# Moving the row sums of a sort's ranks from ScalarE into accumulating VectorE instructions

## The chip, the cores and the metric

One Trainium2 chip, one core of it. The metric is the device time of one execution of the whole kernel in microseconds (us), the median over the runs.

## The reference

12,500 nodes with 64 features and 200,000 edges (`src`, `dst` sorted by `dst`). Two graph layers follow each other, each behind a layer norm and a ReLU. Cut to what matters:

```python
# layer 0
aggr_msg = segment_sum(edge_attr_64, src, num_segments=12500)
x = x + relu(concat([h, aggr_msg]) @ W1 + b1) @ W2 + b2
# layer 1: attention over the edges of each destination
z = h @ W_fc.T
a = z[src] @ blk[0] + z[dst] @ blk[3] + ex @ w_e + (a constant of the moments of z[src], z[dst])
att = where(a > 0, a, 0.01 * a)
w = exp(att - segment_max(att, dst)[dst]); w = w / segment_sum(w, dst)[dst]
x = x + segment_sum(w[:, None] * (z[src] + ez), dst)
```

The change lies in layer 0. Its sum goes over `src`, and the edges are sorted by `dst`, so the kernel first sorts the edges' rows by source.

## The kernel before, in words

Edges are taken in 196 **macros** of 1,024 (128 partitions x `G` = 8 columns). A node is a pair of one of 98 blocks (`NB`) and a place in it. The macros fall into 8 chunks of 8, 20, 34, 38, 34, 26, 20 and 16 (`MS`). Within a chunk every edge gets a row number ("rank") in a sorted table in HBM. GpSimd (POOL) scatters the macro's 64-wide rows there by 8 indirect DMAs, one for each column (`scatter`, line 615). While chunk c is ranked and scattered, the sorted rows of chunk c-1 are read back by SyncE (SP) in groups of four tiles and summed: VectorE builds one-hots (`next_group`, line 1381), TensorE multiplies (`group`, line 990), VectorE adds the four results into `work` (`add`, line 1368). VectorE also builds one-hots to count chunk c+1 (line 1281, counted by TensorE at line 925), and ScalarE builds one-hot-like signs of the destinations (`destination_signs`, 8 + 8 activations at lines 723 and 725), which TensorE multiplies (line 968). All this is one straight-line program per engine, written out macro by macro.

The rank of a macro goes so:

1. TensorE leaves in PSUM (`ranks`, 128 x 8 x 98) a running count for each block (`advance`, lines 956 and 959, `s_rank`). It waits for VectorE's product of the macro before (`s_prod`), since it changes `ranks`.
2. VectorE multiplies `ranks` by the one-hot of each edge's block (`rank`, line 1299, one instruction of 784 columns, `s_prod`). The next instruction is the one-hot of the next macro (line 1281).
3. ScalarE sums each of the eight stretches of 98 products into one number (`rank_out`, line 707, eight activations with an accumulator output, `s_red`), waits for its own `s_red` and converts the eight sums to integers (line 710, `s_idx`). Before it writes `pos_f` and `idx` it waits until the scatter of four macros earlier has landed (`s_sc`).
4. ScalarE then copies the source numbers beside the edge rows (`row_sources`, line 715, `s_col`), and then does the destination signs.
5. POOL waits for `s_idx` and `s_col` and scatters.

`pos_f`, `idx` and `ea_sb` have four buffers, `prod` has two. VectorE waits in `rank(m)` for `s_red` of macro m-2, since it writes that product's buffer. Macro 0 alone is summed and converted by VectorE (lines 1303 and 1306). After the sort come the tail of the sums, the dense layers, and from about 3,000 us on the attention loop, in which POOL gathers (line 643). None of that is touched, but for the name of a semaphore in three waits.

Of the kernel before, what the change touches and what calls it, by code (L numbers as in the profile page):

```python
# [4 lines left out]
ALU = mybir.AluOpType  # L5
# [87 lines left out]
def gnn_kernel(nc, x, src, dst, e2, e64, W1, b1, W2, b2, W_fc, W_attn, W_edge, W_e2n, W_m1, W_m2, out):  # L93
    with ExitStack() as ctx:
# [168 lines left out]
        s_prod = sem("s_prod")  # L263
        s_red = sem("s_red")
        s_sc = [sem(f"s_sc{k}") for k in range(4)]
# [158 lines left out]
        def _(sp):  # L424
# [79 lines left out]
            sp.wait_ge(s_sp, N0)  # L504
            sp.wait_ge(s_red, NM)
            for i in range(GN[NCH - 1]):
# [149 lines left out]
        def _(act):  # L656
# [40 lines left out]

            def rank_out(m):

                if m == 0:  # L700
                    return
                act.wait_ge(s_prod, m + 1)
                if m >= 4:
                    act.wait_ge(s_sc[m % 4], 16 * G * (m // 4))
                for g in range(G):
                    at = prod[:, m % 2, g * NB:(g + 1) * NB]
                    ins = a_.activation(at, at, ACT.Copy, accum_out=pos_f[:, m % 4, g:g + 1])  # L707
                ins.then_inc(s_red, 1)
                act.wait_ge(s_red, m + 1)
                a_.activation(idx[:, m % 4, :], pos_f[:, m % 4, :], ACT.Copy).then_inc(s_idx, 1)  # L710

            def row_sources(m):
# [22 lines left out]
            for m in range(NM):  # L735
                if m in FILLS:
                    zero_fill(*FILLS[m])
                if m == 5:
                    act.wait_ge(s_dsub, 1)
                    a_.activation(squares_a, d_sb[:, :, :], ACT.Square).then_inc(s_sq, 1)  # L740
                if m == 8:
                    act.wait_ge(s_vv, 1)
                    a_.activation(var_sb[:, :], var_sb[:, :], ACT.Sqrt).then_inc(s_std, 1)
                if m == DST_FROM:
                    act.wait_ge(s_split, 3)
                    act.wait_ge(s_const, 2)
                if m == A0[2]:
                    act.wait_ge(s_tabi, 1)
                if m % 2 == 0 and 0 <= m - A0[2] < 18:
                    floor_fill((m - A0[2]) // 2)  # L750
                rank_out(m)
                row_sources(m)
                for d in DSTS.get(m, ()):
                    destination_signs(d)
# [455 lines left out]
        def _(dve):  # L1210
# [83 lines left out]
            def rank(m):  # L1294

                dve.wait_ge(s_rank, m + 1)
                if m >= 2:
                    dve.wait_ge(s_red, m - 1)
                v_.tensor_tensor(prod[:, m % 2, :].rearrange("p (h c) -> p h c", h=2), ranks,  # L1299
                                 ohs[:, m % 2, :].rearrange("p (h c) -> p h c", h=2), ALU.mult).then_inc(s_prod, 1)  # L1300
                if m == 0:
                    dve.wait_ge(s_prod, 1)
                    v_.tensor_reduce(pos_f[:, 0, :], prod[:, 0, :].rearrange("p (g j) -> p g j", g=G), X_AXIS, ALU.add
                                     ).then_inc(s_red, 1)
                    dve.wait_ge(s_red, 1)
                    v_.tensor_copy(idx[:, 0, :], pos_f[:, 0, :]).then_inc(s_idx, 1)
                if m + 1 < NM:
                    rank_onehots(m + 1)
# [245 lines left out]
            past = tmp_row[0:1, 0:n].rearrange("a (i u) -> a i u", u=GRP)  # L1554
            dve.wait_ge(s_red, NM)
            ch(v_.tensor_copy(past, at_first))
# [16 lines left out]
            dve.wait_ge(s_add, GRP * N0 + GN[NCH - 1])  # L1573
            dve.wait_ge(s_red, NM)
            dve.sem_inc(s_h, 1)
# [346 lines left out]
```

## Time and profile before

| | us |
|---|---|
| median of 3 runs | 5434.41 (5429.04 to 5434.47) |
| the profiled execution, its own time | 5417.05 |
| its span | 5415.2 |
| first rank product of VectorE (line 1299) starts / last starts | 32.4 / 2717.1 |
| VectorE busy / ScalarE busy / POOL busy / TensorE busy, share of the span | 55% / 41% / 56% / 42% |

Busy time is the union of an engine's instructions; "idle before" a group is what the engine waited ahead of it, and the arrow names what ended the wait. "remote" is a wait whose releaser the profile does not find. "issue" is time in which the engine waited for nothing that the profile shows.

### The profile page before, as it was taken

Reading aid. Unit: us, or ns where it says so; the run is one execution under the profiler, and the core shown is the slowest. Engines: PE = TensorE matmul, PEld = TensorE weight load, DVE = VectorE, ACT = ScalarE, POOL = GpSimd, SP = SyncE. Lnnn points to the kernel's source line nnn. Section 1 sums busy time; section 2 is a strip of 40 time slices with the busy share of each in tenths; the row PEclk is TensorE's granted clock in tenths of the full one; section 3 lists DMA queues with packets and bytes.
Section 4 is the critical chain, followed back from the end, with each engine's and each line's share of the span. In section 5 each row is a group of like instructions: output and inputs, shape, how many; then the busy total and the mean of one; then the engine's idle time right before and its main releaser. Section 6 shows DMA issues by size and latency. Waiting matters only on the chain.

```text
span 5415.2 us, 60061 instructions
## 1 busy us (share of the span) xinstructions
PE 2284.4 (42%) x12501; PEld 1870.7 (35%) x12502; DVE 2997.1 (55%) x9197; ACT 2240.7 (41%) x9095; POOL 3005.6 (56%) x3151
## 2 busy tenths in 40 slices
PE   3545444545554555555786422222222222222222
PEld 1333333433444444444675322222222222222222
DVE  8555444445454555555664455555555555555556
ACT  2566666666555554543263222222222222222222
POOL 6556566555545555454503366666666666666662
PEclk9555555555555565555588655555555555555555
DMA  7433222322222232333331111222112221112212
GB/s 217 114 109 83 71 62 64 70 66 67 67 67 68 64 68 67 69 67 69 87 69 35 18 30 30 30 30 30 30 29 30 30 30 29 29 30 30 30 30 64
DMA packets 726919, 308.40 MB, mean 57 GB/s; under 512 B 661869, under 2 KB 662029, under 8 KB 726480
## 3 DMA queue, kind: packets, MB, share of 16 engines
q1 hardware_dynamic: 612608, 160.26, 14.9%
q0 software_dynamic: 100032, 105.80, 9.6%
q10 hardware_dynamic: 13968, 39.17, 2.1%
q14 instruction: 235, 1.93, 0.1%
q8 instruction: 76, 1.25, 0.1%
HBM read 206.21 MB, written 98.73 MB: 56 GB/s over the span
## 4 chain that ended last, share of the span: by engine, by line
issue 26%; another core or an unknown queue 25%; DVE 25%; ACT 12%; PE 10%; DVEq 2%; DMA 0%; SPq 0%; POOL 0%; ACTq 0%; POOLq 0%
PE half_banks L990 4%; DVE work L1368 4%; ACT z_sb L707 3%; ACT ohp L723 3%; ACT ohj L725 3%; DVE oh_all L1281 2%; DVE work L1784 2%; DVE work L1776 2%; ACT half_banks L842 2%; DVEq L1357 1%; DVE zg L1381 1%; PE half_banks L1158 1%; PE half_banks L1008 1%; DVE tab L1802 1%
## 5 line engine op out<-in xcount | busy, mean ns | idle before, releaser
L615 POOL DMA_INDIRECT sorted_dram<-ea_sb,idx x1563 | 1515.2, 969 | 1194.8 <-ACT ea_sb L715 704.1
L643 POOL DMA_INDIRECT zg<-z_dram,idx x1563 | 1482.8, 949 | 968.7 <-issue 906.2
L990 PE MATMUL half_banks<-z_sb,zg 128*128 128x65 f32 x4280 | 903.7, 385 | 834.7 <-DVE work L1368 616.7
L990 PEld LDWEIGHTS half_banks<-z_sb,zg 128*128 128x128 f32 x4280 | 872.5, 299 | 977.1 <-DVE zg L1381 759.3
L1368 DVE TENSOR_TENSOR work<-work,half_banks 128x65 f32 x2140 | 463.7, 217 | 1004.6 <-remote 806.9
L1169 PE MATMUL low_banks<-ident,f_top 128*80 128x128 f32 x196 | 85.5, 436 | 1465.7 <-DVE f_top L1787 1415.4
L723 ACT ACTIVATE ohp<-trow,zg 128x128 bf16<-128x128 f32 x1568 | 478.1, 386 | 378.9 <-remote 297.2
L707 ACT ACTIVATE z_sb<-z_sb 128x98 f32<-128x98 f32 x1560 | 420.8, 271 | 503.6 <-issue 262.9
L842 ACT ACTIVATE half_banks<-half_banks,f_s 128x80 f32<-128x80 f32 x1568 | 357.5, 316 | 616.8 <-issue 469.7
L1169 PEld LDWEIGHTS low_banks<-ident,f_top 128*80 128x80 f32 x196 | 28.0, 143 | 1503.7 <-DVE f_top L1787 1451.8
L725 ACT ACTIVATE ohj<-trow,zg 128x98 bf16<-128x98 f32 x1568 | 464.2, 364 | 149.9 <-issue 147.9
L1795 DVE SCALAR_TENSOR_TENSOR half_banks<-r_sb,low_banks 80x64 f32<-80x64 f32 x196 | 56.9, 290 | 781.3 <-remote 767.6
L850 ACT ACTIVATE f_fact<-f_ratio 80x2 f32<-80x2 f32 x196 | 39.8, 203 | 1065.5 <-DVE f_ratio L1765 733.3
L1177 PE MATMUL low_banks<-zg,work 128*80 128x68 f32 x3136 | 455.0, 340 | 2.2 <-ACT work L854 2.2
L1381 DVE TENSOR_TENSOR zg<-half_banks,away 128x256 f32<-128x256 f32 x1070 | 446.1, 418 | 2.0 <-issue 1.2
L1177 PEld LDWEIGHTS low_banks<-zg,work 128*80 128x80 f32 x3136 | 441.6, 253 | 2.4 <-ACT work L854 2.4
L1281 DVE TENSOR_TENSOR oh_all<-half_banks,sj_all 128x784 bf16<-128x784 f32 x392 | 377.5, 966 | 25.3 <-remote 14.9
L707 ACT ACTIVATION_READ_ACCUMULATOR z_sb<-z_sb 128x1 f32 x1560 | 293.8, 188 | 116.3 <-issue 116.3
L1299 DVE TENSOR_TENSOR z_sb<-low_banks,oh_all 128x784 f32<-128x784 f32 x196 | 190.0, 969 | 159.1 <-remote 127.9
L968 PE MATMUL half_banks<-ohj,ohp 128*128 128x98 bf16 x1568 | 157.8, 276 | 240.0 <-remote 174.6
L1787 DVE TENSOR_REDUCE f_top<-work 128x80 f32<-128x640 f32 x196 | 239.9, 1224 | 6.7
L1171 PE MATMUL low_banks<-ident,f_max 80*128 80x80 f32 x392 | 140.3, 462 | 240.6 <-issue 202.6
(304 smaller groups left out, 3577.5 us busy)
## 6 DMA issues: line engine op xcount, KB each, us to landing
z_sb<-sorted_dram SPq DMA_DIRECT2D x592, 132.0 KB
ea_sb<-in_edge_attr_dram SPq DMA_DIRECT2D x195, 256.0 KB
sorted_dram<-ea_sb,idx POOLq DMA_INDIRECT x1563
zg<-z_dram,idx POOLq DMA_INDIRECT x1563
sorted_dram<-big_b ACTq DMA_DIRECT2D x4, 3333.0 KB
sorted_dram<-big_b ACTq DMA_DIRECT2D x4, 3069.0 KB
f_t<-t_dram SPq DMA_DIRECT2D x196, 40.0 KB
sorted_dram<-big_b ACTq DMA_DIRECT2D x4, 1353.0 KB, 10.9
```

What stands on the lines that cost most here:

```text
L615: g_.indirect_dma_start(out=sorted_dram[BUF[c]][:, :], out_offset=bass.IndirectOffsetOnAxis(ap=idx[0:n, m % 4, g:g + 1], axis=0), in_=ea_s ...
L643: g_.indirect_dma_start(out=zg[0:n, s, g, 0:ZW + 1], out_offset=None, in_=z_dram[:, :], in_offset=bass.IndirectOffsetOnAxis(ap=idx[0:n, s, ...
L707: ins = a_.activation(at, at, ACT.Copy, accum_out=pos_f[:, m % 4, g:g + 1])
L723: a_.activation(ohp[:, s, g, :], iota_h[:, :], ACT.Sign, bias=dst_p[:, d * G + g:d * G + g + 1], scale=-1.0)
L725: ins = a_.activation(ohj[:, s, g * NB:(g + 1) * NB], iota_h[:, 0:NB], ACT.Sign, bias=dst_j[:, d * G + g:d * G + g + 1], scale=-1.0)
L842: ins = a_.activation(f_masks[:, q % 2, g, :], f_masks[:, q % 2, g, :], ACT.Identity, bias=f_s[:, q % 2, g:g + 1])
L990: ins = t_.matmul(banks[4 + n % 2][:, u * AW:(u + 1) * AW], oh_step[:, n % 2, u, :], es_sb[:, n % 4, u, 0:AW], start=True, stop=True)
L1177: ins = t_.matmul(banks[2 + q % 2][0:W, 0:RW], f_probs[:, q % 2, g, :], zg[:, q % SL, g, :], start=(g == 0), stop=(g == G - 1))
L1281: return v_.tensor_tensor(out.rearrange("p (g j) -> p g j", g=G), iota_ps[:, 0:NB].unsqueeze(1).to_broadcast([P, G, NB]), values[:, cols_o ...
L1368: v_.tensor_tensor(row, row, banks[4 + n % 2][:, u * AW:(u + 1) * AW].unsqueeze(1), ALU.add).then_inc(s_add, 1)
L1381: ins = v_.tensor_tensor(oh_step[:, n % 2, 2 * h:2 * h + 2, :], iota_ps.unsqueeze(1).to_broadcast([P, 2, P]), away[:, n % 2, 2 * h:2 * h + ...
L1787: v_.tensor_reduce(f_top[:, :], scores.rearrange("p g n -> p n g"), X_AXIS, ALU.max).then_inc(f_gmax, 1)
```

## The change

For every macro VectorE now does eight instructions of 98 columns instead of one of 784. Each multiplies its stretch of `ranks` by 1.0 and by the one-hot, and writes the stretch's sum into `pos_f` by an accumulator output. VectorE then waits for its own `s_prod`, waits for the scatter of four macros earlier, and converts the eight sums into `idx`. ScalarE's `rank_out` is gone, with the semaphore `s_red`; VectorE no longer waits for ScalarE there.

```diff
-            def rank_out(m):
-
-                if m == 0:
-                    return
-                act.wait_ge(s_prod, m + 1)
-                if m >= 4:
-                    act.wait_ge(s_sc[m % 4], 16 * G * (m // 4))
-                for g in range(G):
-                    at = prod[:, m % 2, g * NB:(g + 1) * NB]
-                    ins = a_.activation(at, at, ACT.Copy, accum_out=pos_f[:, m % 4, g:g + 1])
-                ins.then_inc(s_red, 1)
-                act.wait_ge(s_red, m + 1)
-                a_.activation(idx[:, m % 4, :], pos_f[:, m % 4, :], ACT.Copy).then_inc(s_idx, 1)
...
-                rank_out(m)
                 row_sources(m)
...
                 dve.wait_ge(s_rank, m + 1)
-                if m >= 2:
-                    dve.wait_ge(s_red, m - 1)
-                v_.tensor_tensor(prod[:, m % 2, :].rearrange("p (h c) -> p h c", h=2), ranks,
-                                 ohs[:, m % 2, :].rearrange("p (h c) -> p h c", h=2), ALU.mult).then_inc(s_prod, 1)
-                if m == 0:
...
+                for g in range(G):
+                    at = slice(g * NB, (g + 1) * NB)
+                    ins = v_.scalar_tensor_tensor(out=prod[:, m % 2, at], in0=ranks[:, g // 4, g % 4 * NB:(g % 4 + 1) * NB],
+                                                  scalar=1.0, in1=ohs[:, m % 2, at], op0=ALU.mult, op1=ALU.mult,
+                                                  accum_out=pos_f[:, m % 4, g:g + 1])
+                ins.then_inc(s_prod, 1)
+                dve.wait_ge(s_prod, m + 1)
+                if m >= 4:
+                    dve.wait_ge(s_sc[m % 4], 16 * G * (m // 4))
+                v_.tensor_copy(idx[:, m % 4, :], pos_f[:, m % 4, :]).then_inc(s_idx, 1)
                 if m + 1 < NM:
                     rank_onehots(m + 1)
```

The waits of SP and VectorE for `s_red` at the sort's end are now for `s_prod`.

**VectorE** in a later chunk, around one rank, with the semaphores that each row waits for. Before (`z_sb` holds the products, `low_banks` the ranks, `oh_all` the one-hots, `work` the sums of the sorted rows):

```order
L1368 TENSOR_TENSOR work<-work,half_banks 128x65
L1299 TENSOR_TENSOR z_sb<-low_banks,oh_all 128x784 [waits s_red,s_rank]
L1281 TENSOR_TENSOR oh_all<-half_banks,sj_all 128x784
L1357 TENSOR_LOAD b_i
L1368 ISA [waits s_add,s_sp]
```

Now:

```order
L1352 TENSOR_TENSOR work<-work,half_banks 128x65
L1283 SCALAR_TENSOR_TENSOR z_sb,pos_f<-low_banks,oh_all 128x98 [waits s_rank]
L1283 SCALAR_TENSOR_TENSOR z_sb,pos_f<-low_banks,oh_all 128x98 x7
L1290 CAST idx<-pos_f 128x8 [waits s_sc2,s_prod]
L1265 TENSOR_TENSOR oh_all<-half_banks,sj_all 128x784
L1341 TENSOR_LOAD b_i
L1352 ISA [waits s_add,s_sp]
```

One row has become nine, and the row behind them, the next macro's one-hot, stands behind a wait for a scatter.

**ScalarE** over one macro and the start of the next, at such a place. Before:

```order
L707 ACTIVATE z_sb,pos_f<-z_sb 128x98 [waits s_sc0,s_prod]
L707 ACTIVATE z_sb,pos_f<-z_sb 128x98 x7
L710 ACTIVATE idx<-pos_f 128x8 [waits s_red]
L715 ACTIVATE ea_sb<-ee_sb 128x8 [waits s_ea0]
L723 ACTIVATE ohp<-trow,zg 128x128 [waits s_dst_used]
L723 ACTIVATE ohp<-trow,zg 128x128 x7
L725 ACTIVATE ohj<-trow,zg 128x98 x8
```

Now:

```order
L700 ACTIVATE ea_sb<-ee_sb 128x8 [waits s_ea2]
L708 ACTIVATE ohp<-trow,zg 128x128 [waits s_dst_used]
L708 ACTIVATE ohp<-trow,zg 128x128 x7
L710 ACTIVATE ohj<-trow,zg 128x98 x8
L700 ACTIVATE ea_sb<-ee_sb 128x8 [waits s_ea3]
```

ScalarE no longer waits for VectorE in this stretch; what it hands to POOL (`ea_sb`) still stands behind the destination signs of the macro before.

## Rows read from the trace of the kernel before

**Rows 1.** The page, part 1: busy us, share of the span, instructions of each engine.
```profile
PE 2284.4 (42%) x12501; PEld 1870.7 (35%) x12502; DVE 2997.1 (55%) x9197; ACT 2240.7 (41%) x9095; POOL 3005.6 (56%) x3151
```

**Rows 2.** Busy time in stretches: macros 28 to 61, 134 to 159, and behind the sort.
```profile
core 0: us, PE busy (x) PEld busy (x) DVE busy (x) ACT busy (x) POOL busy (x), PEclk, DMA share, GB/s
399.40:824.60 425.20, 205.20 (x1059) 159.44 (x1057) 204.26 (x649) 281.70 (x1249) 261.62 (x272) 0.55 0.29 70
1815.10:2214.60 399.50, 222.54 (x1144) 186.15 (x1144) 211.30 (x797) 205.39 (x950) 199.87 (x209) 0.57 0.30 68
2724.90:5415.20 2690.30, 866.34 (x5360) 742.21 (x5359) 1554.64 (x4318) 792.04 (x2435) 1484.94 (x1567) 0.54 0.20 33
```

**Rows 3.** Groups of POOL: busy us, mean ns of one, idle before by releaser.
```profile
L615 POOL DMA_INDIRECT sorted_dram<-ea_sb,idx x1563 | 1515.2, 969 | 1194.8 <-ACT ea_sb L715 704.1 <-issue 465.3 <-DVE idx L1306 20.5
```

**Rows 4.** Timeline of POOL, macros 43 to 45: start, us, [idle before].
```profile
587.78 0.95 POOL L615 DMA_INDIRECT sorted_dram<-ea_sb,idx  x1 [4.65 <-ACT ea_sb L715]
...
606.71 0.96 POOL L615 DMA_INDIRECT sorted_dram<-ea_sb,idx  x1 [0.30 <-issue]
613.08 0.96 POOL L615 DMA_INDIRECT sorted_dram<-ea_sb,idx  x1 [5.41 <-ACT ea_sb L715]
```

**Rows 5.** Timeline of ACT, the same stretch.
```profile
591.39 0.27 ACT L707 ACTIVATE z_sb<-z_sb 128x98 f32<-128x98 f32 x1
591.56 0.19 ACT L707 ACTIVATION_READ_ACCUMULATOR z_sb<-z_sb 128x1 f32 x1
591.66 0.27 ACT L707 ACTIVATE z_sb<-z_sb 128x98 f32<-128x98 f32 x1
...
597.69 0.38 ACT L725 ACTIVATE ohj<-trow,zg 128x98 bf16<-128x98 f32 x1 [0.19 <-issue]
...
606.16 0.28 ACT L707 ACTIVATE z_sb<-z_sb 128x98 f32<-128x98 f32 x1 [1.03 <-issue]
...
612.12 0.20 ACT L715 ACTIVATE ea_sb<-ee_sb 128x8 f32<-128x8 f32 x1
```

**Rows 6.** Timeline of DVE, the same stretch.
```profile
588.55 0.97 DVE L1299 TENSOR_TENSOR z_sb<-low_banks,oh_all 128x784 f32<-128x784 f32 x1
...
594.93 0.97 DVE L1299 TENSOR_TENSOR z_sb<-low_banks,oh_all 128x784 f32<-128x784 f32 x1
595.82 0.96 DVE L1281 TENSOR_TENSOR oh_all<-half_banks,sj_all 128x784 bf16<-128x784 f32 x1
609.80 0.22 DVE L1368 TENSOR_TENSOR work<-work,half_banks 128x65 f32 x1 [13.01 <-remote]
```

**Rows 7.** Timeline of DVE, small instructions back to back.
```profile
1502.97 0.16 DVE L1419 TENSOR_REDUCE lo_all<-dst_f 128x2 f32<-128x16 f32 x1
1503.05 0.21 DVE L1368 TENSOR_TENSOR work<-work,half_banks 128x65 f32 x1
1503.17 0.15 DVE L1375 TENSOR_TENSOR away<-z_sb 128x4 f32<-128x4 f32 x1
```

**Rows 8.** Timeline of POOL, first scatters of macros 168 to 170, then of 175 and 176.
```profile
2330.82 0.95 POOL L615 DMA_INDIRECT sorted_dram<-ea_sb,idx  x1 [10.57 <-ACT ea_sb L715]
2342.22 0.96 POOL L615 DMA_INDIRECT sorted_dram<-ea_sb,idx  x1 [1.61 <-ACT ea_sb L715]
2363.42 0.96 POOL L615 DMA_INDIRECT sorted_dram<-ea_sb,idx  x1 [11.41 <-ACT ea_sb L715]
...
2444.68 0.95 POOL L615 DMA_INDIRECT sorted_dram<-ea_sb,idx  x1 [10.44 <-ACT ea_sb L715]
2456.75 0.95 POOL L615 DMA_INDIRECT sorted_dram<-ea_sb,idx  x1 [2.28 <-ACT ea_sb L715]
```

**Rows 9.** Timeline of DVE and ACT at macro 168.
```profile
2326.47 0.97 DVE L1299 TENSOR_TENSOR z_sb<-low_banks,oh_all 128x784 f32<-128x784 f32 x1
...
2327.47 0.28 ACT L707 ACTIVATE z_sb<-z_sb 128x98 f32<-128x98 f32 x1 [8.96 <-DVE z_sb L1299]
...
2329.75 0.21 ACT L710 ACTIVATE idx<-pos_f 128x8 int32<-128x8 f32 x1
```

More of the change, by code:

```diff
@@ L263, in gnn_kernel @@
         s_prod = sem("s_prod")
-        s_red = sem("s_red")
         s_sc = [sem(f"s_sc{k}") for k in range(4)]
@@ L504, in _ @@
             sp.wait_ge(s_sp, N0)
-            sp.wait_ge(s_red, NM)
+            sp.wait_ge(s_prod, NM)
             for i in range(GN[NCH - 1]):
@@ L1296, in rank @@
                 dve.wait_ge(s_rank, m + 1)
-                if m >= 2:
-                    dve.wait_ge(s_red, m - 1)
-                v_.tensor_tensor(prod[:, m % 2, :].rearrange("p (h c) -> p h c", h=2), ranks,
-                                 ohs[:, m % 2, :].rearrange("p (h c) -> p h c", h=2), ALU.mult).then_inc(s_prod, 1)
-                if m == 0:
[L1302 to L1306, printed above, removed]
+                for g in range(G):
[8 more added lines that the diff above has]
+                v_.tensor_copy(idx[:, m % 4, :], pos_f[:, m % 4, :]).then_inc(s_idx, 1)
                 if m + 1 < NM:
@@ L1554, in _ @@
             past = tmp_row[0:1, 0:n].rearrange("a (i u) -> a i u", u=GRP)
-            dve.wait_ge(s_red, NM)
+            dve.wait_ge(s_prod, NM)
             ch(v_.tensor_copy(past, at_first))
@@ L1573, in _ @@
             dve.wait_ge(s_add, GRP * N0 + GN[NCH - 1])
-            dve.wait_ge(s_red, NM)
+            dve.wait_ge(s_prod, NM)
             dve.sem_inc(s_h, 1)
```

## The prediction

> **What bounds the kernel now.** I read the busy shares first [rows 1]: no engine is above 56%, so the time lies in waits between engines, and a faster engine gains only where others wait for it. The stretches [rows 2] say where the change can act. Behind 2,725 us nothing of it is left, and those 2,690 us stay. All of it lies in the sort, 2,725 us for 196 macros, 13.9 us for each.
>
> What the sort must do at least is POOL's: from 587.78 to 606.71 us it starts one scatter every 1.26 us [rows 4], so 8 x 1.26 = 10.1 us for a macro and 1,980 us for 196. Of the rest, 704 us are idle time of POOL that ends with ScalarE's source column (line 715), which ScalarE writes right behind the row sums that the change takes away [rows 3]. That is the case for the change: POOL starves, and what it waits for stands behind ScalarE's row sums.
>
> The timelines say why it starves. POOL runs two macros in one burst, 587.8 to 607.7 us, stops for 5.4 us and begins again at 613.08 [rows 4]. ScalarE works fast in the first part of the burst: from 591.39 a sum takes 0.27 us, the activation and the read of its accumulator together. From 597.69, 9.9 us into the burst, the same ScalarE stalls in "issue" between single instructions: the eight steps to 606.16 take 8.5 us [rows 5]. VectorE works through to 596.8 us and is then held for 13.01 us, to 609.80, for sums of TensorE [rows 6]. **Both are freed 2 to 3 us after POOL's burst ends.** So a cycle of two macros (25.3 us) has a slow phase of some 13 us in which TensorE and ScalarE crawl and VectorE soon stands, and a window of some 12 to 14 us in which they do their work. What the slow phase is I can't say from the rows; it begins about one macro into an unbroken burst. Later it is the same with VectorE the last: at macro 168 ScalarE has waited 8.96 us for the product [rows 9], and POOL 10.57 us [rows 8].
>
> **The change, part by part.**
>
> ScalarE loses eight sums of 0.27 us and a conversion: from 2327.47 to 2329.75 us, 2.28 us, and to the source column 2.4 us [rows 9]. For 195 macros that is 464 us of an engine that is 281.70 of 425.20 us busy in macros 28 to 61 and 205.39 of 399.50 in 134 to 159 [rows 2].
>
> VectorE loses one instruction that holds it for 0.89 us (594.93 to 595.82) [rows 6]. It gets eight of 98 columns. Start to start a 65-column one takes 0.12 us (1503.05 to 1503.17) [rows 7]; between these two the slope is 0.77 / 719 = 1.07 ns a column, and 98 columns take 0.155 us. Does the accumulator cost a second instruction? No row shows one on VectorE. ScalarE's sum is two records, 0.17 us and then 0.10 [rows 5], and VectorE's smallest step here is 0.08 us (1502.97 to 1503.05) [rows 7]. I take 0.155 + 0.08 for each, 1.88 us for eight. The conversion waits for the last sum to end (about 0.1 us, a duration of 0.21 to 0.26 less the step of 0.155) and takes 0.08. **Net: 1.88 + 0.18 - 0.89 = 1.17 us more for a macro.** The bounds: without a second instruction 8 x 0.155 + 0.18 - 0.89 = 0.53 us; with each of the sixteen waiting for the one before, 8 x (0.26 + 0.15) + 0.18 - 0.89 = 2.6 us. I take 1.17, being nearest to ScalarE's own pair.
>
> The Trainium skill, VectorE: DVE Perf Modes, section "Two Vector instructions with no wait between them", says that an operation which also writes out its accumulator is two instructions, the main one and a read. By that rule the 0.53 us falls away as a bound; the trace has such a pair only on ScalarE.
>
> Waits. VectorE no longer waits for `s_red`. It waits instead for the scatter of four macros earlier, and the next macro's one-hot and all sums of sorted rows are queued behind that. ScalarE waited for the same before, and VectorE's rank of macro 44 starts at 594.93, while POOL is at macro 43: a lead of one or two, so this costs nothing. TensorE's `advance` waits for `s_prod`, now 1.0 us later.
>
> The hand-off becomes shorter: from the product's start at 2326.47 to the converted index at 2329.96 it is 3.5 us [rows 9]; now 1.88 + 0.18 + 0.17 = 2.2. POOL can start 1.3 us earlier where VectorE comes last. Where ScalarE comes last it is 2.4 us.
>
> **The sum.** Macros 104 to 195, paced by VectorE and TensorE: 92 x 1.17 = +108 us. Each of some 46 bursts starts 1.3 us earlier, -60 us at most; but an earlier burst also brings the slow phase earlier and takes from VectorE's window what POOL gains, so I count half, -30. Net +78. Macros 9 to 103: 47 cycles of about 25 us. ScalarE's 2.4 us before each burst go, -113 us at most. VectorE needs from rank to rank 6.4 us at its fastest (588.55 to 594.93) [rows 6]; two macros are 12.8 us of a window of 12 to 14. With 2.34 us more they are 15.1, so 1.1 to 2.3 us a cycle must come from a longer stop, +52 to +110 us. Of ScalarE's gain not all is left: once it keeps up, POOL runs longer bursts, in which the slow phase is longer. I take 85 us for each, so 0, less 5 us at the sort's last rank, where the shorter hand-off counts in full. Macros 0 to 8 are POOL's or the set-up's, 0. Together **+73 us on the profiled execution's 5417: 5490.** The median of the runs lies 17 us above it, so I predict a median of 5505 (rounded).
>
> **The rivals.**
>
> *ScalarE was the brake (faster).* If VectorE's window has room in macros 9 to 103, POOL's stops shrink by ScalarE's 2.4 us: -113 us there; with +78 later that is -35, and with the full -60 in the later macros -65: 5370 to 5400. For it: 704 us of POOL's idle time end with ScalarE, and VectorE is only 48% busy in macros 28 to 61. Against it: VectorE is held through the slow phases. Chance 0.18.
>
> *A slower VectorE spreads the scatters (faster).* At macros 175 and 176 the starts are 12.07 us apart with 2.28 us between bursts; at 168 to 170, with only 1.61 us between, two macros take 32.6 us [rows 8]. If 1.17 us more open that gap, macros 134 to 179 run at about 13 us each instead of 15.4 (399.5 / 26) [rows 2]: -110 us. With +108 x 46 / 92 = +54 for the other later macros, less 30, and -5: 5434 - 91 = 5345. Against it: the index of a burst's second macro now comes a little sooner, which closes the same gap. Chance 0.12.
>
> *VectorE is on the path everywhere (slower).* 187 x 1.17 = +219: 5650; at the upper bound 187 x 2.6 = +486: 5920. It decides if VectorE is the last in every cycle and nothing is won at the hand-off. Chance 0.15.
>
> *Nothing comes of it.* The gain at the hand-off equals the loss: within 0.2% of 5434 (11 us, about what a measurement of this kernel can tell from no change). Chance 0.10.
>
> My forecast, a loss of some 20 to 140 us, has 0.45: its own range is 5455 to 5575. Faster is 0.30, same 0.10, slower 0.60. The range for 8 in 10 is 5370 to 5610: it leaves out the spread-out scatters' full gain and most of the case with VectorE everywhere.
>
> The Trainium skill has a rule that speaks against this change: VectorE: DVE Perf Modes, section "The TRN2 errata", says that many small tiles pay the latency between instructions once for each, and a large one once. In this trace the fixed part is 0.12 - 65 x 0.00107 = 0.05 us a step [rows 7], 0.4 us for eight, and it is in the sum.
>
> **What would show it.** In the profile after, eight rows of 98 columns start to start 0.15 to 0.25 us apart, with or without a read between them, and a rank that holds VectorE for 1.9 to 2.1 us. ScalarE's busy time near 2240 - 460 = 1780 us. POOL's stops before bursts longer in macros 104 to 195, and bursts of three macros in 28 to 99. The sort ends near 2,800 us instead of 2,725; what follows stays at 2,690 us. I am wrong if POOL's idle time falls below 1,195 us, if POOL's starts come in even steps of 12 to 13 us, or if VectorE's long waits (13 us) vanish with ScalarE's load.

## The result, and the profile after

| | before | after |
|---|---|---|
| median of 4 runs each | 5431.73 us | 5497.72 us |
| lowest to highest | 5423.4 to 5434.47 | 5492.99 to 5503.23 |
| profiled execution, span | 5415.2 us | 5501.4 us |
| last scatter ends (end of the sort) | 2724.9 us | 2810.5 us |
| behind the sort | 2690.3 us | 2690.9 us |

The ratio is 1.0124, with a 95% interval of 1.0107 to 1.0142: slower by 66 us. The forecast was 5505 us. The total comes out right, and the terms that it is added up from do not, which the profile and the runs show below.

The page of the kernel after, parts 1 and 4 (the latter is the chain of work that ended last, by engine), and part 4 of the kernel before:

```profile
PE 2372.0 (43%) x12501; PEld 1903.2 (35%) x12502; DVE 3145.3 (57%) x12331; ACT 1723.4 (31%) x5780; POOL 3000.5 (55%) x3151
...
DVE 32%; another core or an unknown queue 25%; issue 25%; PE 9%; ACT 4%; DVEq 3%; DMA 1%; SPq 0%; ACTq 0%; POOL 0%; POOLq 0%
```
```profile
issue 26%; another core or an unknown queue 25%; DVE 25%; ACT 12%; PE 10%; DVEq 2%; DMA 0%; SPq 0%; POOL 0%; ACTq 0%; POOLq 0%
```

Against [rows 1] ScalarE loses 517 us of busy time and VectorE gains 148. In both kernels a quarter of the chain hangs on something that the profile can't name. Keep that figure in mind: it is what sets this set of runs apart from later ones.

The same stretches of macros as in [rows 2], in the kernel after:

```profile
core 0: us, PE busy (x) PEld busy (x) DVE busy (x) ACT busy (x) POOL busy (x), PEclk, DMA share, GB/s
409.20:876.10 466.90, 210.86 (x1074) 153.56 (x1073) 230.69 (x1212) 182.25 (x661) 260.37 (x272) 0.55 0.27 65
1877.10:2280.60 403.50, 234.12 (x1139) 190.29 (x1137) 227.62 (x1208) 139.81 (x507) 199.03 (x208) 0.54 0.30 67
2810.50:5501.40 2690.90, 866.16 (x5368) 742.43 (x5367) 1556.66 (x4324) 792.01 (x2435) 1484.88 (x1567) 0.54 0.21 33
```

Macros 28 to 61 take 466.9 us in place of 425.2, and macros 134 to 159 take 403.5 in place of 399.5. The loss is early, where I had forecast none, and hardly anything is lost late, where I had forecast 78 us. By the starts of POOL's first scatters, macros 9 to 103 lose about 80 us and macros 104 to 195 about 10.

The groups of instructions of the kernel after (busy us, mean ns of one | idle before, by releaser), for POOL's scatters [rows 3], VectorE's accumulating rank with its second instruction, the new conversion on VectorE, and ScalarE's signs:

```profile
L614 POOL DMA_INDIRECT sorted_dram<-ea_sb,idx x1563 | 1510.2, 966 | 1285.5 <-issue 469.6 <-DVE idx L1290 416.4 <-ACT ea_sb L700 399.2
L1283 DVE SCALAR_TENSOR_TENSOR z_sb<-low_banks,oh_all 128x98 f32<-128x98 f32 x1568 | 298.0, 254 | 134.3 <-remote 94.3 <-PE low_banks L943 19.5 <-issue 19.2
L1283 DVE DVE_READ_ACCUMULATOR z_sb<-low_banks,oh_all 128x1 f32 x1568 | 130.3, 83 | 14.0 <-issue 13.9
L1290 DVE CAST idx<-pos_f 128x8 int32<-128x8 f32 x196 | 35.3, 180 | 121.8 <-remote 92.7 <-DVE z_sb L1283 17.5 <-issue 6.3
L708 ACT ACTIVATE ohp<-trow,zg 128x128 bf16<-128x128 f32 x1568 | 478.5, 387 | 1501.3 <-remote 862.5 <-PE half_banks L952 448.8 <-issue 189.8
```

ScalarE, relieved, now idles 1501.3 us ahead of its signs. POOL's idle time grew from 1194.8 to 1285.5 us. The 704.1 us that ended with ScalarE's source column became some 400, and 416 us now end with VectorE's index. And VectorE stands 121.8 us ahead of the new conversion, a wait that my sum does not hold (the expectations below call it 117 us, which is the part with a named end).

How long a rank holds VectorE, on its timeline (start, duration) at one macro:

```profile
1524.58 0.26 DVE L1283 SCALAR_TENSOR_TENSOR z_sb<-low_banks,oh_all 128x98 f32<-128x98 f32 x1
1524.76 0.08 DVE L1283 DVE_READ_ACCUMULATOR z_sb<-low_banks,oh_all 128x1 f32 x1
...
1526.01 0.09 DVE L1283 DVE_READ_ACCUMULATOR z_sb<-low_banks,oh_all 128x1 f32 x1
1526.13 0.17 DVE L1290 CAST idx<-pos_f 128x8 int32<-128x8 f32 x1
1526.21 0.97 DVE L1265 TENSOR_TENSOR oh_all<-half_banks,sj_all 128x784 bf16<-128x784 f32 x1
```

The accumulator is a second instruction, but its start coincides with that of the next main one: 0.18 us a pair, not 0.235. From the first sum to the next one-hot it is 1526.21 - 1524.58 = 1.63 us, where [rows 6] has 595.82 - 594.93 = 0.89. The change costs VectorE **0.74 us for each macro**, not 1.17.

A few microseconds earlier, TensorE's sums, VectorE's wait for them, and POOL's scatters around that wait, from the timelines of PE, DVE and POOL:

```profile
1504.08 1.00 PE L974 MATMUL half_banks<-z_sb,zg 128*128 128x65 f32 x8
...
1506.16 1.08 PE L974 MATMUL half_banks<-z_sb,zg 128*128 128x65 f32 x8 [0.74 <-issue]
```
```profile
1505.80 0.21 DVE L1352 TENSOR_TENSOR work<-work,half_banks 128x65 f32 x1
1521.37 0.22 DVE L1352 TENSOR_TENSOR work<-work,half_banks 128x65 f32 x1 [15.36 <-remote]
```
```profile
1500.07 0.96 POOL L614 DMA_INDIRECT sorted_dram<-ea_sb,idx  x1 [7.14 <-ACT ea_sb L700]
...
1519.00 0.96 POOL L614 DMA_INDIRECT sorted_dram<-ea_sb,idx  x1 [0.30 <-issue]
1526.58 0.96 POOL L614 DMA_INDIRECT sorted_dram<-ea_sb,idx  x1 [6.62 <-DVE idx L1290]
```

VectorE adds the sums of a group only after it has prepared the next one, so it waits here for the eight matmuls whose records stand at 1504.08 to 1505.08 us, not for those at 1506.16. It goes on at 1521.37, 16 us later and 1.4 us after POOL's burst of two macros has ended. This is the slow phase of the prediction. It is now seen for what it does: work that is in the records already becomes known to the waiting engine many microseconds late. VectorE itself is not slow to notice: the semaphore's last two recorded updates are at 1501.88 and at 1521.24, and VectorE starts 0.13 us behind the latter. Whether the matmuls end late or their update arrives late can't be told, since ends of matmuls are modelled and some updates are missing from the trace.

### The profile page after: what moved, and what is told of

Read it like the earlier page. It is cut to its first block, busy times and chain, and to the rows that moved or that the text cites. A ratio compares the mean times of both kernels' runs of the same rounds, so it can differ in the third digit from the quotient of the medians.

```text
span 5501.4 us, 59688 instructions
## 1 busy us (share of the span) xinstructions
PE 2372.0 (43%) x12501; PEld 1903.2 (35%) x12502; DVE 3145.3 (57%) x12331; ACT 1723.4 (31%) x5780; POOL 3000.5 (55%) x3151
## 4 chain that ended last, share of the span: by engine, by line
DVE 32%; another core or an unknown queue 25%; issue 25%; PE 9%; ACT 4%; DVEq 3%; DMA 1%; SPq 0%; ACTq 0%; POOL 0%; POOLq 0%
DVE work L1352 7%; DVE z_sb L1283 5%; PE half_banks L974 3%; DVE work L1768 2%; DVE work L1760 2%; ACT half_banks L826 2%; DVEq L1341 2%; DVE zg L1365 2%; DVE oh_all L1265 2%; PE half_banks L1142 1%; PE half_banks L992 1%; DVE tab L1786 1%; DVE tab L1754 1%; DVE away L1359 1%
## 5 line engine op out<-in xcount | busy, mean ns | idle before, releaser
L614 POOL DMA_INDIRECT sorted_dram<-ea_sb,idx x1563 | 1510.2, 966 | 1285.5 <-issue 469.6
L974 PE MATMUL half_banks<-z_sb,zg 128*128 128x65 f32 x4280 | 961.4, 402 | 799.4 <-DVE work L1352 518.5
L974 PEld LDWEIGHTS half_banks<-z_sb,zg 128*128 128x128 f32 x4280 | 903.3, 312 | 990.0 <-DVE zg L1365 648.4
L708 ACT ACTIVATE ohp<-trow,zg 128x128 bf16<-128x128 f32 x1568 | 478.5, 387 | 1501.3 <-remote 862.5
L710 ACT ACTIVATE ohj<-trow,zg 128x98 bf16<-128x98 f32 x1568 | 439.5, 361 | 17.1 <-issue 16.9
L1283 DVE SCALAR_TENSOR_TENSOR z_sb<-low_banks,oh_all 128x98 f32<-128x98 f32 x1568 | 298.0, 254 | 134.3 <-remote 94.3
L940 PE MATMUL low_banks<-oh_all,rest_b 128*128 128x392 bf16 x376 | 153.4, 510 | 326.2 <-DVE oh_all L1265 279.2
L1155 PEld LDWEIGHTS low_banks<-ident,f_max 80*128 80x128 f32 x392 | 98.1, 310 | 294.5 <-issue 238.7
L1768 DVE SCALAR_TENSOR_TENSOR work<-half_banks,work 128x640 f32<-128x640 f32 x196 | 161.7, 825 | 45.7 <-ACT work L830 29.4
```

The source lines that it names most:

```text
L614: g_.indirect_dma_start(out=sorted_dram[BUF[c]][:, :], out_offset=bass.IndirectOffsetOnAxis(ap=idx[0:n, m % 4, g:g + 1], axis=0), in_=ea_s ...
L708: a_.activation(ohp[:, s, g, :], iota_h[:, :], ACT.Sign, bias=dst_p[:, d * G + g:d * G + g + 1], scale=-1.0)
L710: ins = a_.activation(ohj[:, s, g * NB:(g + 1) * NB], iota_h[:, 0:NB], ACT.Sign, bias=dst_j[:, d * G + g:d * G + g + 1], scale=-1.0)
L974: ins = t_.matmul(banks[4 + n % 2][:, u * AW:(u + 1) * AW], oh_step[:, n % 2, u, :], es_sb[:, n % 4, u, 0:AW], start=True, stop=True)
L1283: ins = v_.scalar_tensor_tensor(out=prod[:, m % 2, at], in0=ranks[:, g // 4, g % 4 * NB:(g % 4 + 1) * NB], scalar=1.0, in1=ohs[:, m % 2, a ...
L1768: v_.scalar_tensor_tensor(out=scores, in0=f_masks[:, q % 2, :, :], scalar=SLOPE, in1=scores, op0=ALU.mult, op1=ALU.max).then_inc(f_leaky, 1)
```

## The experiments

The runs were made on several chips, each set on one. In the first set the kernel before took 5497.36 us (median of 7, against 5431.73 us in the result), and **4241.66, 4241.67 and 4241.88 us on three others**. All ratios below are to the kernel before on the same chip. The expected times of the first set were written for a kernel before at 5432 us, and are best read as ratios to it. The two kinds of chip have to be kept apart, since on the second kind the slow phase isn't there at all. These four sets ran on four different chips, so whether the chip itself or something else at that time makes the difference is not shown; "kind of chip" is a name for what the kernel before takes there.

### Which part of the change costs (chip with before at 5497 us)

**Seven index buffers.** Theory A says that VectorE's new wait for a free index buffer is what costs; theory B is the forecast's, the longer rank in a window between slow phases.

```diff
-                if m >= 4:
-                    dve.wait_ge(s_sc[m % 4], 16 * G * (m // 4))
-                v_.tensor_copy(idx[:, m % 4, :], pos_f[:, m % 4, :]).then_inc(s_idx, 1)
+                if m >= SL:
+                    dve.wait_ge(s_sc[(m - SL) % 4], 16 * G * ((m - SL) // 4 + 1))
+                v_.tensor_copy(idx[:, m % SL, :], pos_f[:, m % 4, :]).then_inc(s_idx, 1)
...
-                        out_offset=bass.IndirectOffsetOnAxis(ap=idx[0:n, m % 4, g:g + 1], axis=0),
+                        out_offset=bass.IndirectOffsetOnAxis(ap=idx[0:n, m % SL, g:g + 1], axis=0),
```

> The kernel after, with seven index buffers in place of four: VectorE's conversion waits for the scatter of seven macros earlier. In the trace after, VectorE stands 117 us before its conversions (92.7 us of it ends with 'remote'). Theory A (the new wait for a free index buffer costs this): those 117 us go, and the time is 5380 to 5440 us. Theory B (VectorE stands there for its own product, in the slow phase that POOL's bursts bring, and the buffer has long been free): the 117 us stay within 20, and the time is 5498 us within 10.

Measured: 5567.21 us, ratio 1.0155 (1.0119 to 1.0190). The conversion's group in its trace:

```profile
L1290 DVE CAST idx<-pos_f 128x8 int32<-128x8 f32 x196 | 35.5, 181 | 130.4 <-remote 95.6 <-DVE z_sb L1283 26.9 <-issue 3.0
```

With a buffer that has been free for three macros more, VectorE stands there as long as in the kernel after (130.4 us of idle time, 95.6 of it "remote", against 121.8 and 92.7 in the result). Theory A falls. The trace of the kernel after says the same: whenever VectorE stands over 1 us there, POOL's last scatter of four macros earlier had been issued at least 23 us before that wait began. The other thing that the conversion waits for is VectorE's own last sum, and it is this update that comes late: 42 of the 44 waits of over 0.5 us end within 0.2 us behind a recorded update of `s_prod`.

This kernel also stands in for the kernel after in what follows, since the latter was not itself run on this chip: 5567.21 us is what the next runs are compared with.

**VectorE's part alone.** The kernel before, with the eight accumulating instructions in place of the product; their sums go to a spare tile, and ScalarE still sums and converts.

```diff
-                v_.tensor_tensor(prod[:, m % 2, :].rearrange("p (h c) -> p h c", h=2), ranks,
-                                 ohs[:, m % 2, :].rearrange("p (h c) -> p h c", h=2), ALU.mult).then_inc(s_prod, 1)
+                for g in range(G):
+                    at = slice(g * NB, (g + 1) * NB)
+                    ins = v_.scalar_tensor_tensor(out=prod[:, m % 2, at], in0=ranks[:, g // 4, g % 4 * NB:(g % 4 + 1) * NB],
+                                                  scalar=1.0, in1=ohs[:, m % 2, at], op0=ALU.mult, op1=ALU.mult,
+                                                  accum_out=pos_v[:, m % 4, g:g + 1])
+                ins.then_inc(s_prod, 1)
```

> The kernel before, but VectorE multiplies and sums in the eight accumulating instructions (sums into a spare tile), while ScalarE still sums and converts as before. VectorE's part of the change alone. Theory B (VectorE's longer rank narrows its window between slow phases, ScalarE's load matters little): the rank is 0.5 us longer (no conversion on VectorE), and the index comes 0.5 us later: 5465 to 5510 us, loss mostly in macros 9 to 103. Theory C (ScalarE's relief gave back much of what VectorE lost): more than the kernel after, 5520 to 5580 us.

Measured: 5545.40 us, ratio 1.0103 (1.0083 to 1.0124). VectorE's longer rank alone gives most of the loss of the change: 48 us (within 11) of the 70 (within 20) that the kernel with seven buffers loses on this chip. The 22 us between them are hardly more than the noise; what they hold beyond it goes with the conversion on VectorE, which this kernel lacks. Theory C, that ScalarE's relief gives much of it back, expected this kernel above the kernel after, and it is below.

**ScalarE's sums kept.** The kernel after, with ScalarE's eight sums and conversion back in their old place ahead of the source column, into spare tiles.

```diff
+                act.wait_ge(s_prod, m + 1)
+                for g in range(G):
+                    at = prod[:, m % 2, g * NB:(g + 1) * NB]
+                    ins = a_.activation(at, at, ACT.Copy, accum_out=pos_v[:, m % 4, g:g + 1])
+                ins.then_inc(s_red, 1)
+                act.wait_ge(s_red, m)
+                a_.activation(idx_v[:, m % 4, :], pos_v[:, m % 4, :], ACT.Copy)
...
                 dve.wait_ge(s_rank, m + 1)
+                if m >= 3:
+                    dve.wait_ge(s_red, m - 2)
```

> The kernel after, with ScalarE's eight row sums and conversion kept where they were, into spare tiles (nobody but the reuse of the product waits for them). The source column of a macro is again 2.4 us later. Theory B (ScalarE's relief brought nothing): 5498 us within 15. Theory C (relief was worth the 85 us of the forecast in macros 9 to 103): 5560 to 5600 us, with POOL's idle time ending with the source column back at 700 us from 379.

Measured: 5563.84 us, ratio 1.0129 (1.0100 to 1.0157), the same as the kernel with seven buffers on this chip (5567.21 us) and as the ratio of the result (1.0124) within the intervals, which are 16 to 20 us wide to either side. Theory C asked for 1.024 to 1.031. And yet in its waits POOL's idle time ends with the source column for twice as long as in the kernel with seven buffers, whose row stands first:

```profile
L614 POOL DMA_INDIRECT sorted_dram<-ea_sb,idx x1563 | 1516.4, 970 | 1299.0 <-issue 466.0 <-DVE idx L1290 435.2 <-ACT ea_sb L700 397.1
```
```profile
L617 POOL DMA_INDIRECT sorted_dram<-ea_sb,idx x1563 | 1515.8, 970 | 1306.2 <-ACT ea_sb L715 800.7 <-issue 458.3 <-DVE idx L1308 42.4
L1308 DVE CAST idx<-pos_f 128x8 int32<-128x8 f32 x196 | 36.6, 187 | 136.2 <-remote 108.9 <-DVE z_sb L1301 20.4 <-issue 2.2
```

Some 400 us of POOL's idle time changed their name from "VectorE's index" to "ScalarE's source column", and the time did not change. **The 704 us of [rows 3], the whole case for the change, were the name of the last in a queue of late engines, not the price of its work.**

**The conversion back on ScalarE.** The kernel after, sums on VectorE, conversion on ScalarE, so that VectorE never waits for its own sum. Before it overwrites `pos_f` VectorE must now wait for ScalarE's conversion of four macros earlier; in the trace none of VectorE's waits of over 0.5 us ahead of a rank ends with that.

```diff
+                if m >= 4:
+                    dve.wait_ge(s_idx, m - 3)
...
-                dve.wait_ge(s_prod, m + 1)
-                if m >= 4:
-                    dve.wait_ge(s_sc[m % 4], 16 * G * (m // 4))
-                v_.tensor_copy(idx[:, m % 4, :], pos_f[:, m % 4, :]).then_inc(s_idx, 1)
...
+                act.wait_ge(s_prod, m + 1)
+                if m >= 4:
+                    act.wait_ge(s_sc[m % 4], 16 * G * (m // 4))
+                a_.activation(idx[:, m % 4, :], pos_f[:, m % 4, :], ACT.Copy).then_inc(s_idx, 1)
```

> The kernel after, with the conversion on ScalarE (as before) and the sums on VectorE: VectorE has neither the wait for its own product nor the wait for the buffer, 0.15 to 0.25 us less for each macro in the fast part, and 117 us of stalls less at most. Theory A or B's variant (the conversion on VectorE is what costs): 5400 to 5450 us. Theory B as in the forecast (it is the window, and a held VectorE would be held at its next wait anyway): 5460 to 5495 us.

Measured: 5597.21 us, ratio 1.0188 (1.0170 to 1.0206): worse than either, against both expectations. ScalarE's conversion waits 873.0 us, of them 644.5 for VectorE:

```profile
L614 POOL DMA_INDIRECT sorted_dram<-ea_sb,idx x1563 | 1520.4, 973 | 1340.0 <-ACT ea_sb L707 863.4 <-issue 469.1 <-ACT idx L702 4.4
L702 ACT ACTIVATE idx<-pos_f 128x8 int32<-128x8 f32 x196 | 39.5, 202 | 873.0 <-DVE z_sb L1293 644.5 <-remote 169.8 <-issue 58.7
```

The 121.8 us that VectorE stands at its conversion are thus not saved by moving the conversion. The likely reason, which these rows fit but no further run tested: a wait that goes over to another engine is exposed to late updates too, and holds up what is queued there (the source column, with which 863.4 us of POOL's idle time now end).

### Whether POOL's bursts make the updates late (chips with before at 4242 us)

**A stop between macros.** POOL starts a macro only when the one before has landed, in the kernel after and in the kernel before:

```diff
             def scatter(c, m):

+                if m:
+                    pool.wait_ge(s_sc[(m - 1) % 4], 16 * G * ((m - 1) // 4 + 1))
                 pool.wait_ge(s_idx, m + 1)
```

> The kernel after, but POOL starts the scatters of a macro only when the scatters of the macro before have landed (1.8 us after the last issue in the trace), so no burst is longer than 8 scatters. Theory B (TensorE's and ScalarE's updates come late only from about 9 us into an unbroken burst, and that sets the pace): the late updates go, VectorE's waits of over 1.5 us with them, POOL's starts come in steps of 12.2 to 13 us: the sort takes 2450 to 2600 us in place of 2810, the kernel 0.94 to 0.97 of before on the same chip. Rival D (the bursts are not the cause, POOL's time counts): about 70 joins of bursts get 2 us each, +140 us: 1.03 to 1.04 of before.

> The kernel before with the same wait for the macro before. Theory B: 0.94 to 0.97 of before, within 0.005 of the kernel after with it, since POOL then paces both and VectorE's 0.7 us for each macro are hidden. Rival D: 1.03 to 1.04.

Measured: 4540.57 us (1.0707, 1.0689 to 1.0725) and 4531.96 us (1.0687, 1.0669 to 1.0704). No theory foresaw this size, because none foresaw a chip on which before takes 4242 us. The second kernel was run on two more chips.

> The kernel before with POOL's wait for the macro before to land, unchanged from the earlier run, where it cost 6.9% on a chip on which before took 4242 us. Where before takes 5430 to 5500 us. Theory B (unbroken bursts of 9 us and more make TensorE's updates late): steps of 11.5 to 12.5 us, the sort 2300 to 2500 us, 0.93 to 0.96 of before. Rival E (the chip delays updates whatever POOL does): the stops come on top, 1.03 to 1.08. Where before takes 4242 us: 1.069 again.

> The kernel before with POOL's wait for the macro before to land, once more, in the hope of a chip where before takes 5430 to 5500 us. There, theory B: 0.93 to 0.96; rival E (the chip delays updates whatever POOL does): 1.03 to 1.08. Where before takes 4240 us: 1.069 again, which tells nothing new.

Measured: 1.0694 (1.0677 to 1.0712) and 1.0697 (1.0679 to 1.0715), again beside a kernel before at 4241.67 and 4241.88 us. Where updates come in time a stop costs its own length and gives nothing: the pauses ahead of macros add up to 352.8 us in the kernel before with a stop and to 64.3 without (its trace is below), and the sort ends at 2324.4 us in place of 2032.1. Whether it would help where they come late was not tried: all three chips were of the second kind.

**The two kernels on such a chip, with traces.**

> The kernel after, unchanged. The kernel before took 5432, 5497 and 4242 us in the three sets of runs so far, so its ratio is asked for on another chip. Where before takes about 5430 to 5500 us (the sort at 13.9 us for each macro, updates of TensorE late): 1.012 again, 1.010 to 1.015. Where before takes about 4240 us (the sort then takes 4242 - 2204 = 2038 us, 10.4 us for each macro, POOL's own pace): VectorE's 0.74 us for each macro are hidden behind POOL, 0.998 to 1.005.

> The kernel before, unchanged, for its trace. Ratio 1.000. On a chip where it takes about 4240 us: one unbroken burst of POOL over nearly the whole sort, 10.14 us for each macro up to the end (the kernel after shows 10.63 and 10.48 us in macros 160 to 179 and 180 to 194), a sort of about 2035 us, and updates of TensorE that come at once. On a chip where it takes 5430 to 5500 us: updates late and stops as in the first trace.

Measured: the kernel after 4267.12 us, ratio 1.0058 (1.0042 to 1.0075); the kernel before 4240.42 us, ratio 0.9998 (0.9988 to 1.0007). So the change makes the kernel slower on both kinds of chip, here by 25 us. The chain of work that ended last, then POOL's group, in the kernel before:

```profile
POOL 45%; issue 19%; PE 12%; DVE 10%; ACT 7%; DMA 4%; DVEq 1%; POOLq 0%; SPq 0%; ACTq 0%
```
```profile
L615 POOL DMA_INDIRECT sorted_dram<-ea_sb,idx x1563 | 1515.6, 970 | 501.7 <-issue 461.6 <-DVE idx L1306 20.5 <-ACT ea_sb L715 18.9
```

The quarter of the chain that had no name is gone, and so is the idle time that ended with ScalarE: 18.9 us in place of 704.1, with the same program. Behind the first few macros POOL's scatters run in one burst of 190 macros, with no stop of over 0.4 us, and no wait in the whole trace ends with "remote"; in the kernel after none does there either. **So an unbroken burst is not enough to bring the slow phase**, which the prediction took as its law.

Stretches of both kernels there: first before, macros 134 to 159, 160 to 179 and 180 to 194, then after, the same macros.

```profile
1410.00:1673.80 263.80, 223.06 (x1140) 185.47 (x1140) 209.62 (x792) 198.56 (x944) 200.39 (x209) 0.58 0.46 102
1673.80:1877.10 203.30, 169.88 (x909) 143.27 (x909) 169.70 (x651) 145.47 (x708) 154.52 (x160) 0.62 0.49 106
1877.10:2028.60 151.50, 143.13 (x584) 123.77 (x584) 121.88 (x516) 35.85 (x252) 114.95 (x120) 0.50 0.50 108
```
```profile
1411.90:1675.90 264.00, 226.65 (x1130) 185.11 (x1131) 225.43 (x1191) 136.07 (x496) 200.57 (x209) 0.56 0.46 102
1675.90:1888.40 212.50, 188.46 (x904) 156.35 (x901) 182.06 (x950) 95.87 (x349) 154.61 (x161) 0.54 0.48 102
1888.40:2045.50 157.10, 138.99 (x553) 115.97 (x553) 127.69 (x723) 2.81 (x13) 115.05 (x120) 0.50 0.48 101
```

Up to macro 159 both go at POOL's pace, 263.8 / 26 = 10.15 us, and VectorE's 0.74 us are hidden. From macro 160 on the kernel after needs 10.63 and then 10.47 us where before needs 10.17 and 10.10. In these traces the sort ends at 2032.1 and 2049.0 us (+16.9), and behind the last scatter before has 2207.0 us and after 2218.6 (+11.6), together the 28.5 us between the two spans. The second part is the same debt: with POOL's last scatter done, VectorE of the kernel before has no sums of sorted rows left to add, while that of the kernel after has 20 and ends them 9.5 us later. My expectation of 0.998 to 1.005 missed this: I had not asked how little room VectorE has behind POOL at the end.

**Half the scatters.** To see VectorE's price with POOL out of the way, every second scatter of a macro is left out in both kernels (their outputs lack those rows), and the landing counts are halved.

```diff
-                for g in range(G if m < NM - 1 else LG + 1):
+                for g in range(0, G, 2) if m < NM - 1 else range(LG + 1):
```

> The kernel before with every second scatter left out (four of a macro's eight; its output lacks those rows), so that POOL needs 5 us for a macro. Theory B: no burst reaches 9 us, updates are prompt, and VectorE paces the sort with 8 to 10 us for each macro: 1600 to 1950 us for the sort. Rival D (TensorE and VectorE need their 13 us without POOL's doing): the sort stays above 2400 us.

> The kernel after with every second scatter left out in the same way. Where VectorE paces, its longer rank counts for each macro: start to start of rank and next one-hot 1.63 us against 0.89, so +0.74 x 187 = +138 us over the other half kernel. If ScalarE's relief were worth something where POOL is out of the way, less than 100 us.

Measured: 3938.75 us (0.9284, 0.9268 to 0.9299) and 4000.66 us (0.9432, 0.9416 to 0.9447), so the change costs 62 us, not the 138 that I expected. The sort ends at 1725.0 and 1780.3 us, in the range of theory B and far below rival D's 2400; but since updates are in time on this chip whatever POOL does, this decides nothing about bursts where they are late. Macros 28 to 61 and 134 to 159, first of before, then of after:

```profile
300.30:558.70 258.40, 189.12 (x1056) 146.98 (x1056) 199.79 (x648) 257.33 (x1237) 130.91 (x136) 0.62 0.42 98
1127.70:1374.20 246.50, 203.60 (x1140) 170.47 (x1140) 208.90 (x793) 199.67 (x950) 99.59 (x105) 0.65 0.46 96
```
```profile
306.20:546.00 239.80, 196.31 (x1065) 144.36 (x1062) 222.46 (x1193) 181.51 (x662) 130.39 (x137) 0.63 0.47 108
1141.10:1404.40 263.30, 231.96 (x1140) 190.15 (x1140) 227.01 (x1209) 139.41 (x508) 99.73 (x104) 0.55 0.42 90
```

These four rows hold both effects of the change in the open. In macros 28 to 61 ScalarE is the bound of the kernel before, busy for 257.33 of 258.40 us, and its relief, less what VectorE's longer rank takes, is worth 18.6 us (258.4 to 239.8). In macros 134 to 159 no engine is the bound alone (VectorE 208.90, PE 203.60, ScalarE 199.67 of 246.50), the relief is worth next to nothing, and the change costs 16.8 us, 0.65 for each macro; by the starts of the scatters it is 0.61 in macros 100 to 133 and 0.76 in 180 to 194. So VectorE's 0.74 us lie nearly whole on the path from about macro 100 on, and ScalarE's load is on it only ahead of that, and only when POOL does not pace. One thing more differs in macros 134 to 159: the granted clock of TensorE is 0.65 in the kernel before and 0.55 in the one after, and PE is busy 28.4 us more. No run holds the clock equal. Against it as the cause stands VectorE's idle time, which it would have to lengthen: 37.6 us before (246.50 less 208.90) and 36.3 after, so that VectorE's own 18.1 us of busy time account for the whole difference.

## Why the prediction was right, and where it was not

- **"Net: 1.17 us more for a macro."** The right kind of cost, its size too large: 0.74 us. The second instruction exists, as I took it, but read and next main instruction start together, so a pair is 0.18 us and not 0.155 + 0.08. The term is mis-sized by 0.43 us a macro. The rank holds VectorE for 1.63 us; I had written 1.9 to 2.1.
- **"ScalarE loses eight sums ... 464 us."** It lost 517 us (2240.7 to 1723.4, forecast 1780).
- **"ScalarE's 2.4 us before each burst go, -113 us at most ... I take 85 us."** This step failed. On one chip the kernel with ScalarE's sums kept takes 5563.84 us and the one without them (seven buffers) 5567.21: the relief is worth nothing that can be measured, where 85 us would have stood out from an uncertainty of some 25 for their difference. I had read 704 us of idle time that ended with line 715 as partly ScalarE's doing. On another chip the same program has 18.9 us of it.
- **The wait for the scatter of four macros earlier, costed at nothing.** Right: with seven buffers VectorE stands there as long. But the conversion's other wait, for VectorE's own last sum, I had costed as 0.1 us. It is 6.8 us in all where updates are in time, and 121.8 us (92.7 of it "remote") in the trace of this result.
- **"Macros 104 to 195 ... net +78", "Macros 9 to 103: ... so 0".** Each was wrong by about as much as the other, and they cancelled: about +10 and +80 were measured. Late, the even spread of one of my rivals came in part: the first scatters of macros 109 to 112 and of 115 to 119 start 11.8 to 12.0 us apart, and macros 100 to 133 take 13.92 us each in place of 14.34. Early, POOL's bursts of three macros came as written (17 in the sort in place of 3, six of them in macros 28 to 61), each with a longer stop behind it, and nothing was there to set against VectorE's longer rank. That the longer rank is what costs is shown (VectorE's part alone gives 1.0103); why it costs early and hardly late where updates are late is not.
- **"Both are freed 2 to 3 us after POOL's burst ends ... it begins about one macro into an unbroken burst."** It holds for about two thirds of the cases in both traces of the result: of VectorE's waits of over 5 us behind 200 us, 56 of 88 before and 39 of 59 after end up to 4.2 us behind a burst of POOL (1.4 us in the rows above), the others inside a burst. As a law it is wrong: a burst of 190 macros elsewhere brings none. What makes updates late on some chips, and whether POOL's bursts are a condition there or only coincide, stays open.
- **"The sort ends near 2,800 us ... what follows stays at 2,690."** 2810.5 and 2690.9.

Of the signs that I named for being wrong, POOL's idle time rose instead of falling, as forecast (1285.5 from 1194.8); even steps of 12 us appeared at seven macros. A sign for being right did not come: POOL's stops of over 1 us in macros 104 to 195 add up to 454 us in place of 447, and grew instead in macros 9 to 103, from 282 to 364.

The direction was right for the right reason: it rests on the one term that is confirmed on both kinds of chip, that VectorE has more to do for each macro. The size, 66 us against a forecast of some 71, is luck: VectorE's term was too large, ScalarE's gain did not exist, and early and late errors of nearly 80 us each cancelled. With updates in time the same change costs 25 us. The runs found no version that is faster than the kernel before.

## What to carry to other kernels

Work moved from a light engine to the one that paces costs nearly its full length wherever that engine comes last (here 0.61 to 0.76 us of 0.74), and the relief of the other counts only where that one is the bound; ask for each stage which is which (a share of 257 in 258 us is a bound, a long idle row that ends with an engine is not). "Waited for X" names who came last, and when all are late for a common reason the name moves from one to the next without a microsecond gained. An idle row that ends with "remote" in a program on one core is a warning: here it stood for something that three other chips did not show. Take a second trace on another chip before you build a model on it.

## What the runs showed of the hardware

The kernel before took 5417 us in the profiled execution on one chip and 4241 us on another, with TensorE's mean granted clock at 0.563 and 0.576 of full speed and nearly the same busy times (POOL 3005.6 and 3008.5 us, VectorE 2997.1 and 3000.4). The difference lies in waits, in both halves: 693 us in the sort (2724.9 against 2032.1) and 483 us behind it (2690.3 against 2207.0). In the slower one engines wait for updates of work whose records have long ended, 16 us in the rows above. TensorE's are the worst (VectorE's "remote" waits in the sort of the kernel before, 964 us in all, end with them), but ScalarE's come late too (175 us of TensorE's waits there), and so do VectorE's own (160 us in the kernel after). I had taken this for a property of the kernel.

VectorE's DVE_READ_ACCUMULATOR has a duration of 83 ns, and the next main instruction starts at the same time as it: eight multiply-and-sum instructions of 98 float32 columns pass in 8 x 0.18 us, against 0.89 us for one product of 784 columns without sums.
